# Grouping an attention-and-experts kernel's score matmuls by TensorE array mode, with the values product in a shared ring of banks and a fully unrolled program

## The reference

```python
h = layernorm(x) * (1 + ca) + sa
q, k, v = heads(h @ wq + bq), heads(h @ wk + bk), heads(h @ wv + bv)   # 16 heads of 16
attn = softmax(q @ k.T * scale)                                       # 16 x 512 x 512 per batch
x = x + ga * ((attn @ v) @ wo + bo)
h = layernorm(x) * (1 + cb) + sb
shared = gelu(h @ up_s) @ down_s                                      # 2 experts, 128 wide
gate = top 4 of softmax(h @ router.T) over 16 experts, zero elsewhere
routed = (gelu(h @ up_r) * gate) @ down_r                             # 16 experts, 128 wide
x = x + gb * (shared + routed)
```

## Time and profile before

| | |
|---|---|
| median of 3 runs | 1054.28 us (1052.84 to 1055.86) |
| profiled execution | 1056.11 us |
| its span in the profile | 1054.3 us |
| PE busy | 944.9 us (90%) |
| DVE busy | 680.8 us (65%) |
| ACT busy | 630.9 us (60%) |
| POOL busy | 380.2 us (36%) |
| chain that ended last | PE 78%, DVE 9%, ACT 3%, issue 3%, DMA 2%, POOL 2% |

### The profile page before, as it was taken

How to read it: one execution, slowest core, us unless ns; L and a number is a source line. 1 busy time by engine, 2 the same in 40 slices (tenths; PEclk the granted TensorE clock), 3 DMA queues, 4 the chain that set the end, 5 groups by cost and what they waited for, 6 DMA issues and landing times.

```text
span 1054.3 us, 17394 instructions
## 1 busy us (share of the span) xinstructions
PE 944.9 (90%) x5928; PEld 423.4 (40%) x5928; DVE 680.8 (65%) x1315; ACT 630.9 (60%) x1033; POOL 380.2 (36%) x325
## 2 busy tenths in 40 slices
PE   5468887899999999999999899999999999997897
PEld 3112222234444354444434354444444444345564
DVE  5675576766876677676866676676866667724333
ACT  3145553676675758666776657666675757662343
POOL 4331222232432434243434333243434332344354
PEclk9657988899999999999999998999999999999899
DMA  6810600172016210442017200452017100320130
GB/s 208 180 45 29 117 2 0 46 168 101 1 36 170 68 61 11 140 83 101 1 42 191 85 20 1 123 110 101 1 36 195 64 19 1 111 65 37 66 122 21
DMA packets 50428, 78.53 MB, mean 74 GB/s; under 512 B 8216, under 2 KB 44568, under 8 KB 46240
## 3 DMA queue, kind: packets, MB, share of 16 engines
q1 hardware_dynamic: 50336, 77.36, 27.0%
HBM read 64.31 MB, written 12.89 MB: 73 GB/s over the span
## 4 chain that ended last, share of the span: by engine, by line
PE 78%; DVE 9%; ACT 3%; issue 3%; DMA 2%; POOL 2%; SPq 1%; DVEq 0%; POOLq 0%; ACTq 0%
PE scalar_bank L840 21%; PE down_bank L978 20%; PE pv_bank L912 12%; PE vector_bank L889 12%; DVE neg_max L783 5%; PE scalar_bank L889 5%; PE vector_bank L840 4%; PE scalar_bank L923 2%; PE vector_bank L931 2%; ACT probs L591 1%; DVE rows L657 1%; POOL act_lo L547 1%; PE vector_bank L896 1%; DMA probs<-in_router 1%; DVE o_raw L830 1%
## 5 line engine op out<-in xcount | busy, mean ns | idle before, releaser
L783 DVE TENSOR_REDUCE neg_max<-vector_bank 128x1 f16<-128x512 f32 x512 | 339.7, 688 | 140.2 <-PE vector_bank L889 130.4
L591 ACT ACTIVATE probs<-scalar_bank 128x512 f32<-128x512 f32 x512 | 291.1, 603 | 207.4 <-PE scalar_bank L889 204.6
L547 POOL TENSOR_TENSOR act_lo<-gelu,act_hi 128x512 f16<-128x512 f32 x144 | 178.0, 1256 | 202.8 <-ACT act_hi L581 192.9
L889 PE MATMUL vector_bank<-k_aug,q_aug 64*128 64x512 f16 x512 | 193.6, 411 | 40.7 <-DVE neg_max L783 23.3
L889 PE MATMUL scalar_bank<-q_aug,k_aug 64*128 64x512 f16 x512 | 199.4, 404 | 8.4 <-ACT f_ring L564 3.7
L978 PE MATMUL down_bank<-down_hi,act_hi 128*128 128x256 f16 x576 | 163.2, 283 | 0.3
L978 PE MATMUL down_bank<-down_lo,act_hi 128*128 128x256 f16 x576 | 159.6, 277 | 0.0
L978 PE MATMUL down_bank<-down_hi,act_lo 128*128 128x256 f16 x576 | 159.4, 277 | 0.0
L773 DVE TENSOR_TENSOR gelu<-gelu,gates 128x512 f32<-128x512 f32 x128 | 113.1, 903 | 61.8 <-ACT gelu L636 60.1
L912 PE MATMUL pv_bank<-probs,v_aug 128*32 128x512 f32 x1024 | 135.0, 639 | 0.0
L636 ACT ACTIVATE gelu<-scalar_bank 128x512 f32<-128x512 f32 x144 | 85.2, 597 | 78.5 <-PE scalar_bank L840 56.4
(11 more groups left out here) (122 smaller groups left out, 1107.9 us busy)
## 6 DMA issues: line engine op xcount, KB each, us to landing
gates<-gates_by_expert SPq DMA_DIRECT2D x32, 1024.0 KB, 5.1
q_aug<-q_parts SPq DMA_DIRECT2D x48, 128.0 KB, 3.9
k_aug<-k_parts SPq DMA_DIRECT2D x48, 128.0 KB, 7.5
x_pre<-in_x SPq DMA_DIRECT2D x8, 512.0 KB, 6.4
x_post<-in_x SPq DMA_DIRECT2D x8, 512.0 KB, 4.1
out<-x_post SPq DMA_DIRECT2D x8, 512.0 KB, 3.2
gates<-in_w_up SPq DMA_DIRECT2D x4, 576.0 KB, 11.7
gates<-in_w_down SPq DMA_DIRECT2D x4, 576.0 KB, 5.4
```

Source lines behind the costliest of these rows:

```text
L547: pool.tensor_tensor(act[1][:, c, :], gelu[:, n % NGELU, :], act[0][:, c, :], ALU.subtract).then_inc(s_elo, 1)
L591: scalar.activation(probs[:, n % U, :], src[:], ACT.Exp, scale=SCALE).then_inc(taken[kind], 1)
L783: dve.tensor_reduce(neg_max[:, (u // 2) % TT, at:at + 1], src[:], AX.X, ALU.max, negate=True).then_inc(done, 1)
L889: pe.matmul(dst[:], st[at:at + 64, pair, t * P:(t + 1) * P], mo[at:at + 64, pair, :], start=True, stop=True).then_inc(sig, 1)
```

## The change

In `slot_order`, `NO_MAX` goes. At every odd u the two `max` of units u-1 and u are issued together, behind them the two `exp`, and then all `down` items that have fallen due. No `max` is left in the up phase, where `maxT` comes one `up` earlier. The next slot's two early `exp` stand together behind the last `up`, and the four `pv` together behind them. An item `oraw` says where DVE copies the result. `OB` goes, the vector ring has three banks in place of two, and the four `pv` of a slot take one of these as a member of the ring. All eleven bodies are written out. `EXTRAS`, the SP program's order, and every computation stay.

```diff
-NO_MAX = {0: (3, 5, 8), 1: (0, 11, 12), 2: (0, 10), 3: (0, 15)}
 def slot_order(s):
     out = []
     maxima = [("max", (s + 1) * U + u) if s < 3 else ("max0", u) for u in range(U)]
+    early = [("exp", (s + 1) * U + u) if s < 3 else ("exp0", u) for u in range(EARLY)]
...
     for u in range(U):
         out += EXTRAS.get((s, u), [])
-        if u not in NO_MAX[s]:
-            out.append(maxima.pop(0))
-        if u >= EARLY:
-            out.append(("exp", s * U + u))
+        if u % 2:
+            out += maxima[u - 1:u + 1]
+            out += [("exp", s * U + v) for v in (u - 1, u) if v >= EARLY]
...
     for j, up in enumerate(ups):
         out += EXTRAS.get((s, U + j), [])
-        if j == 3:
-            out += maxima + [("maxT", s + 1) if s < 3 else ("maxT0", 0)]
-            maxima = []
+        if j == 2:
+            out.append(("maxT", s + 1) if s < 3 else ("maxT0", 0))
         out.append(up)
-        if j < 2:
-            out += maxima[:2]
-            maxima = maxima[2:]
         if j >= 1:
             out.append(("gated", up[1] - 1))
-        if j >= 3:
-            out.append(("pv", s * TT + j - 3))
+    out += early
     out.append(("gated", ups[-1][1]))
-    for kc in range(len(ups) - 3, TT):
-        out.append(("pv", s * TT + kc))
-        if kc >= TT - EARLY:
-            out.append(("exp", (s + 1) * U + kc - TT + EARLY) if s < 3 else ("exp0", kc - TT + EARLY))
+    out += [("pv", s * TT + kc) for kc in range(TT)]
+    out.append(("oraw", s))
     return out
...
-NV, NRB = 2, 3
+NV, NRB = 3, 3
...
-    seq = [item for _, item in ORDER if item[0] in kinds]
+    seq = [item for _, item in ORDER if item[0] in kinds or is_pv_bank(item) and kinds is V_KINDS]
...
-        OB = ctx.enter_context(nc.psum_tensor("pv_bank", [P, S], F32))
...
         def iterations(eng, body):
-            for i in (-1, 0, 1, 2):
-                body(i, i % 2)
-            with eng.Fori(0, 2) as j:
-                body(j * 2 + 3, 1)
-                body(j * 2 + 4, 0)
-            for i in (7, 8, 9):
+            for i in range(-1, B + 2):
                 body(i, i % 2)
...
+                        if kind == "oraw":
+                            wait(dve, made["pv"], G * TT, b, TT * (n + 1))
+                            wait(dve, made["oT"], 4, b, 0)
+                            dve.tensor_copy(o_raw[:, n, :], bank(("pv", n * TT))[:]).then_inc(taken["pv"], 1)
...
                             if kc == 0:
                                 if g == 0:
                                     wait(pe, taken["v"], 2, b, 2)
-                                wait(pe, taken["pv"], 4, b, g)
+                                wait_bank(pe, ("pv", n), i)
...
-                                o = OB[32 * j:32 * j + 32, :]
+                                o = bank(("pv", g * TT))[32 * j:32 * j + 32, :]
```

More of the change, by code:

```diff
@@ L129, in true_item, with is_pv_bank @@
         return kind, n, -2
-    return kind, n, 0 if kind in ("max", "maxT", "exp", "pv", "xg") else -1
+    return kind, n, 0 if kind in ("max", "maxT", "exp", "pv", "oraw", "xg") else -1
+def is_pv_bank(item):
+    return item[0] == "pv" and item[1] % TT == 0
 def ring(kinds, banks):
-    seq = [item for _, item in ORDER if item[0] in kinds]
+    seq = [item for _, item in ORDER if item[0] in kinds or is_pv_bank(item) and kinds is V_KINDS]
     seq += [None] * (-len(seq) % banks)
@@ L297, in bank @@
             n = RINGS[item][0]
-            return (VB if kind in V_KINDS else RB)[n]
+            return (VB if kind in V_KINDS or kind == "pv" else RB)[n]
         def wait_bank(eng, item, i):
@@ L305, in wait_bank @@
                 if exists(b) or (not isinstance(i, int)):
-                    wait(eng, taken[kind], PER[kind], b, n + 1)
+                    if kind == "pv":
+                        wait(eng, taken["pv"], G, b, n // TT + 1)
+                    else:
+                        wait(eng, taken[kind], PER[kind], b, n + 1)
                     return
         def iterations(eng, body):
-            for i in (-1, 0, 1, 2):
-                body(i, i % 2)
-            with eng.Fori(0, 2) as j:
-                body(j * 2 + 3, 1)
-                body(j * 2 + 4, 0)
-            for i in (7, 8, 9):
+            for i in range(-1, B + 2):
                 body(i, i % 2)
@@ L668, in _ @@
             ln_rows(x_pre, mv[0], rstd[0], s_ln1, s_rs1, 0)
-            src, src2 = (m[:, 0:8 * B].rearrange("p (k b) -> p b k", k=8) for m in (DB[0], OB))
+            src = DB[0][:, 0:8 * B].rearrange("p (k b) -> p b k", k=8)
             dve.wait_ge(s_setup_mm, 1)
@@ L687, in _ @@
             for n, add in ((0, 0.0), (2, 1.0), (4, 0.0), (6, 1.0)):
-                dve.tensor_scalar(tmod_st[:, :, n:n + 2], (src if n < 4 else src2)[:, :, n:n + 2], add, None, ALU.add).then_inc(s_setup_v, 1)
+                dve.tensor_scalar(tmod_st[:, :, n:n + 2], src[:, :, n:n + 2], add, None, ALU.add).then_inc(s_setup_v, 1)
             g = DB[1][0:B, 0:2 * D]
@@ L825, in body @@
                             dve.tensor_copy(gate_rows, src[0:NR, :]).then_inc(done, 1)
-                    if exists(i):
-                        wait(dve, made["pv"], G * TT, i, TT * (s + 1))
-                        wait(dve, made["oT"], 4, i, 0)
-                        dve.tensor_copy(o_raw[:, s, :], OB[:]).then_inc(taken["pv"], 1)
             iterations(dve, body)
@@ L849, in modulations @@
                             for c in range(DC):
-                                o = (DB[0] if k < 2 else OB)[:, (2 * k + half) * B:(2 * k + half + 1) * B]
+                                o = DB[0][:, (2 * k + half) * B:(2 * k + half + 1) * B]
                                 ins = pe.matmul(o, wmod_st[:, c, col + P * half:col + P * half + P], silu[:, c, :],
```

## The result

| | before | after |
|---|---|---|
| median, us | 1053.56 (4 runs) | 1018.97 (4 runs, 1016.42 to 1020.69) |
| ratio | | 0.966, 95% interval 0.9631 to 0.9689 |
| profiled execution, us | 1056.11 | 1016.42 |
| its span, us | 1054.3 | 1014.6 |

What follows compares the result with a forecast made beforehand. PE's work was taken as the bound, with DVE near its limit in slots 0 and 1. Terms 36.5 + 6 + 8 + 3 + 7.3 = 61 us off 1056.1 gave 995, forecast 994, own range 980 to 1008.

Steps and rivals of the forecast that it cites:

- beats: PE's score products: two blocks in opposite array halves cost one beat of 0.215 us; 18 fewer per iteration, 3.9 us.
- signs of being wrong: Middle iterations: slots 0 and 1 over 31 us, slot 1 under 28, or slot 1's granted clock repeatedly under 1.00.
- the walk: Pricing slots 0 to 3 item by item: 27.8, 30.5, 27.8 and 22.5 us, 7.3 us less per iteration.
- The unrolled program: At the loop's turn: writing out all bodies removes 5.2 + 2.1 = 7.3 us; the bound is only 5.2.
- The bank: Values product sharing the vector ring, with its copy of `o_raw`: 0; up to 0.7 us a slot if cover were gone.
- rival D: Pairs needing two free banks leave DVE idle: slower, 1061 at 0.3 us per pair, 1128 at 0.6; chance 0.09.
- 30.5 us in place of 30.3: Slot 1 of a full iteration: waits at its start and for banks mean the change brings nothing there.
- rival C: PE's idle gaps lower the clock in slot 1 of six iterations: some 18 us, 1012; chance 0.09.
- 3 us, between 0 and 10: Iteration 0, paced by DVE: gains by the third bank at most, 3 us.
- Iteration 7: No `max` in slot 3 and no projections, so DVE has more room: 8 us less.
- A: PE gets all its saved work because the third bank lets DVE run evenly: 956 to 975; chance 0.13.
- B: Joined maxima add 2 us in slots 0, 1 and 2 as DVE takes most back: 1012 to 1050; chance 0.17.

Runs made afterwards that it cites:

- the run with two banks: Changed order with a vector ring of two banks and a bank of its own for the values product: 1083.55 us.
- the run with the old tail: Changed kernel's paired unit phase, but the kernel before's slot end: values products from the fourth up on, early exp between the last ones, last gated ahead: 1000.63 us.
- router's choice moved (1006.63): Changed kernel with each slot's last gated ahead of the early exp, and the router's choice moved to the start of slot 1's up phase: 1006.63 us.
- `down` early (994.87): Changed kernel with last gated ahead of early exp, router's choice at slot 1's up phase, and nine down items early in slot 1: 994.87 us.
- the run with the old tail there: Changed kernel, but in slots without up items yet the early exp stand behind the third values product, as before the change: 1002.12 us.
- last `gated` first: Changed kernel with a slot's last gated item ahead of the two early exp on ACT, DVE and POOL, PE's order unchanged: 1012.83 us.
- 976.08: The 994.87 us kernel (early down items), plus early exp behind the third values product in slots without up items: 976.08 us.
- 967.18: The 994.87 us kernel (early down items), with all four values products of every slot ahead of the two early exp: 967.18 us.

## Why the prediction was right, and where its size was off

**The direction held.** PE's work is what the time follows, and the saving of work is real: 73 changes of mode and 18 beats an iteration less. The price of a mode change (0.107) and of a beat (0.215) did not have to be corrected. But the forecast with its own range of 980 to 1008 did not come out, and two of its signs of being wrong did: slot 1 over 31, and a granted clock under 1.00 there time after time.

**Slots 0, 2 and 3** came out within 0.2 us of the walk. In slots 0 and 2 that is partly luck. The walk had waits of 1.5 at the four `oT` in slot 0 and of 1.8 at `gateT` in slot 2. The windows of i = 4 show PE idle for 1.07 and 0.71 in all, and neither wait is there. The largest of those that are there was priced at 0, the copy of `o_raw`:

```profile
475.31 0.39 PE L881 MATMUL vector_bank<-k_aug,q_aug 64*128 64x512 f16 x2 [0.82 <-DVE o_raw L770]
```

The rest is time in which PE is busy, some 0.9 above my count of its work in both slots. In slot 3 the wait of 0.3 to 0.6 for the second early `exp` is as forecast.

**The unrolled program** was a term of 7.3, and the kernel before written out gained 7.3. The 5.2 in it is shown. The 2.1 was taken from a slot in which the clock fell, and the clock falls in that slot without the loop too, so that part of the match is luck. For the changed order the same step is worth 14.7, because its loop turn is costlier; the sum holds only in the order in which I took it.

**The bank.** I took 0 for the shared bank of the values product. In the old order the third bank and the shared one together change full iterations by 0. In the changed order PE stands 0.82 in slot 0 and 0.49 in slot 2 for the copy; no run here gives the paired order three banks and one more for the values product, so what that would save is open. The third bank was priced only as a possible 3 us in iteration 0. In the old order it gave 9 us up to the end of iteration 1. And it decides the sign: the run with two banks gave 1083.55, inside the 1061 to 1128 of rival D. The reason given against D, that a third bank keeps one reduction running, is borne out by that run.

**The first term that failed is slot 1, by the clock.** "30.5 us in place of 30.3" was 32.4: 1.9 us short in each of five iterations, 9.5 us. The clock fell in slot 1 of every iteration from i = 2 to 7. In i = 4 PE was busy for 2.77 us at half the clock; an estimate from this is 1.4 us of extra time, and the run with the old tail shows 1.4 for the same 3.4 us. That leaves 30.2 of the 31.6, so by this estimate the walk's 30.5 would have held at full clock. So rival C, which I had given 0.09 and priced at 18 us for the whole run, came true beside the forecast and not in its place. By the time at the lower clock, slot 1 of the full iterations took:

| run | 0 us | 3.4 us | 6.8 us |
|---|---|---|---|
| changed kernel | | 31.6 | 32.3 to 32.8 |
| pairs with the old tail (1000.63) | 29.7 | 31.1 | 32.0 to 32.2 |
| router's choice moved (1006.63) | 28.5 | 30.0 | 30.8 |
| and `down` early (994.87) | 27.9 | 28.8 | 30.2 |

The walk's sum for slot 1 came near by errors that cancel. Its waits were 2.6 at the start, then 1.0, 1.1 and 1.5; the trace has 2.71, 1.00, 0.24 and 0.86, which is 1.4 less, and my count of PE's work was too low, as in slots 0 and 2. `rows2` was assumed "as now", but the early `exp` ahead of the last `gated` moved POOL's last `act_lo` beside it, 2.21 in place of 1.42. And `rows1`, priced at "some 2.9", took 1.38. I had looked at what PE's new order does to PE and DVE, not at what the same list does to ACT and POOL behind it.

**The second term that failed is the fill.** I gave iteration 0 "3 us, between 0 and 10" and iteration 1 six. By the times of the copies of `o_raw`, the changed kernel reached the end of iteration 0 at 149.6 against 148.4 before, 1.2 later, and iteration 1 gained 2.1. The step "DVE's four copies behind `maxT` are needed only at the early `exp`, two or three `up` later" is true only where there are `up` items. In the fill there are none, and the run with the old tail there shows 17 us. With it the end of iteration 1 comes 15.3 us earlier than before, more than the nine of the forecast.

Iteration 7 gave 6.9 of the 8 forecast. The rest of the run, from the last copy of `o_raw` on, was forecast at 0 and took 1.9 more. It takes 107.0 to 107.3 in the three runs with the old order and 108.6 to 109.6 in all that have pairs, so it goes with the order; why is open.

The parts of the profiled executions, 1056.1 to 1016.4: full iterations with the loop's turn 33.8 (forecast 43.8), iteration 1 2.1 (6), iteration 7 6.9 (8), up to the end of iteration 0 minus 1.2 (3), the rest minus 1.9 (0). That is the whole 39.7. It is 21 short of the forecast's 61; the remaining 5 us between 39.7 and the 34.6 of the medians is which executions were profiled.

**The rivals A and B.** A (PE gets all of it) would have had slot 1 under 28. The changed kernel is far from it, and the runs with slot 1's waits filled reach just 27.9. The measured time lies in B's range (1012 to 1050), and slot 1 lost the 2 us that B gives it, but not by B's mechanism: PE's waits for row maxima ahead of score products fell from 67.2 to 46.8, and slots 0 and 2 came out as forecast. In the run with two banks the same waits are 86.9.

## What to carry to other kernels

Group instructions of one array mode, but count first the banks that the group needs in flight: here one bank more was the difference between 35 us faster and 29 slower. Check an order that is tuned for the steady state in the fill of the pipeline too, where the items that cover a wait don't exist yet. And when a shared list of items is reordered for one engine, walk the others through it: `rows2` grew by 0.8 us and `rows1` shrank by 0.8 to 1.6, only by what POOL had beside them. Where PE waits at the same place of every iteration, look at the granted clock there: what it costs comes on top of the wait.

## What the hardware showed that I had not expected

The loop's turn is not a fixed price: PE stood 0.84 and 0.96 for nothing shown in the kernel before, and 3.18 in the changed order with the same loop.

The granted clock fell in slot 1 six times in a row, 2.3 to 4.7 us behind its start: twice while PE stood the 2.7 us for `rows2`, four times between that wait and the end of the 1.0 us wait behind it. In the paired order fewer and later waits went with fewer falls. With the last `gated` first (2.1 and 1.0 us of waiting) it still fell in all of the five full iterations. With the `down` items early (none at the start, 1.1 and 1.0 later) it fell in two, one and one of the five, in the runs at 994.87, 976.08 and 967.18. But the old order, written out, has falls in three of five with 1.8 us of waiting at that place, and in one of five with three banks. Each count is from one profiled execution, so what sets off a fall is argued and not shown.

And four `rows` instructions of DVE took 1.37 us with nothing of POOL beside them, and longer by about as much as POOL's `act_lo` reached into them:

| run | `act_lo` inside `rows2`, us | `rows2`, us |
|---|---|---|
| changed kernel, iteration 1 | 0 | 1.37 |
| kernel before | 0.30 | 1.42 |
| last `gated` first (1012.83) | 0.52 | 1.64 |
| all values products first (967.18) | 0.83 | 1.95 |
| changed kernel | 1.16 | 2.21 |

From 0.30 on, the time is the overlap and 1.05 to 1.12 us. `act_lo` was moved by the order here and not taken out by itself, but it moved both ways, and wherever it reached into them one instruction of the four was long and the other three took 0.40.
